# Moving the residual fold of a layernorm from VectorE to ScalarE

## The reference

```python
def _layernorm(x, axis=-1, eps=1e-5):
    m = jnp.mean(x, axis=axis, keepdims=True)
    v = jnp.var(x, axis=axis, keepdims=True)
    return (x - m) / jnp.sqrt(v + eps)
...
    # x: (16, 2048, 2048) float32
    xn = _layernorm(x, axis=-1)
    x = x + _L0_attn_ref(xn, ...) + _L0_ffn_ref(xn, ...)
# attention: q = xn @ Wq; latent = xn @ Wkv; k, v = latent @ Wk, latent @ Wv; 16 heads,
#   each row sees its last 128 keys and the first 16; out @ Wo
# ffn: hidden + sigmoid(xn @ router + bias) * (gelu(xn @ w1 + b1) @ w2 + b2) for the rows of
#   the top K scores; _L0_ffn_ref returns its input xn with that added
```

## Time and profile before

| | |
|---|---|
| runs | median 7160.39 us of 3 (7156.94 to 7164.64) |
| profiled execution | 7139.36 us |
| its span, slowest core (5) | 7137.5 us |
| spans of the 8 cores | 7086.8 to 7137.5 us |
| busy, share of the span | PE 82%, DVE 28%, ACT 14%, POOL 2% |
| mean granted PE clock, by core | 0.862 to 0.866 of full speed |

### The profile page before, as it was taken

One profiled execution on the slowest core, in us unless ns is written; L12 is line 12 of the kernel. 1 busy time (PEld: TensorE's weight loads), 2 busy tenths in 40 slices (PEclk: granted clock), 3 DMA queues, 4 the chain that ended last, 5 costly groups with the idle time before them and its releaser, 6 DMA issues.

```text
span 7137.5 us, 105085 instructions; the slowest of 8 cores (7086.8 to 7137.5 us)
## 1 busy us (share of the span) xinstructions
PE 5835.5 (82%) x37961; PEld 3597.9 (50%) x37961; DVE 1995.4 (28%) x4806; ACT 1028.1 (14%) x2688; POOL 160.1 (2%) x155
## 2 busy tenths in 40 slices
PE   2446675868996899968996899967998789977999
PEld 1124343535664366724674357643765356643667
DVE  2033000145113531136112431136212451135211
ACT  0012000104100211004101120104011031103110
POOL 2101011000000000000000000000000000000000
PEclk8656888986998789986998889986999879987999
DMA  9999999721443234431443224431444214431344
GB/s 117 106 122 121 150 154 129 195 89 57 151 150 128 72 119 151 156 107 59 148 152 133 89 95 150 149 128 41 150 152 160 89 69 151 149 128 60 134 145 160
DMA packets 449713, 885.86 MB, mean 124 GB/s; under 512 B 202880, under 2 KB 305856, under 8 KB 400064
## 3 DMA queue, kind: packets, MB, share of 16 engines
q1 hardware_dynamic: 152864, 587.61, 24.3%
q0 software_dynamic: 268704, 90.20, 14.3%
q10 hardware_dynamic: 27648, 201.34, 8.0%
HBM read 935.69 MB, written 123.73 MB: 148 GB/s over the span
## 4 chain that ended last, share of the span: by engine, by line
PE 66%; DMA 16%; DVE 10%; issue 6%; ACT 1%; DVEq 1%; POOL 0%; SPq 0%; ACTq 0%; POOLq 0%
PE ps_ev L826 12%; PE ps_ev L852 12%; DMA w_s<-w_t 6%; PE ps_sB L826 6%; PE ps_sA L826 6%; PE ps_sB L852 6%; PE ps_sA L852 6%; PE ps_ev L786 3%; DMA wq_s<-wq_t 3%; PE ps_ev L572 3%; DMA wk_s<-wk_t 3%; DVE negmax L683 2%; PE ps_sB L786 1%; PE ps_sA L786 1%; DVE p_sb L703 1%
## 5 line engine op out<-in xcount | busy, mean ns | idle before, releaser
L852 PE MATMUL ps_ev<-w_s,hT 128*128 128x256 bf16 x8192 | 957.7, 276 | 158.2 <-DMA w_s<-w_t 127.3
L863 DVE SCALAR_TENSOR_TENSOR acc<-ps_ev,gcol,acc 128x256 f32<-128x256 f32 x512 | 247.9, 484 | 2638.8 <-PE ps_ev L852 2638.8
L852 PEld LDWEIGHTS ps_ev<-w_s,hT 128*128 128x128 bf16 x8192 | 807.5, 99 | 284.3 <-issue 181.8
L826 PE MATMUL ps_ev<-xnT,w_s 128*128 128x512 bf16 x4096 | 911.2, 381 | 34.9 <-DMA w_s<-w_t 34.7
L826 PEld LDWEIGHTS ps_ev<-xnT,w_s 128*128 128x128 bf16 x4096 | 401.9, 98 | 516.8 <-issue 45.4
L826 PE MATMUL ps_sB<-xnT,w_s 128*128 128x512 bf16 x2048 | 472.5, 385 | 36.3 <-DMA w_s<-w_t 36.3
L838 ACT ACTIVATE hT<-ps_ev,b1T 128x512 bf16<-128x512 f32 x256 | 175.9, 687 | 2229.7 <-PE ps_ev L826 2229.6
L852 PE MATMUL ps_sA<-w_s,hT 128*128 128x256 bf16 x4096 | 489.0, 273 | 0.0
L852 PE MATMUL ps_sB<-w_s,hT 128*128 128x256 bf16 x4096 | 489.0, 273 | 0.0
L826 PE MATMUL ps_sA<-xnT,w_s 128*128 128x512 bf16 x2048 | 466.9, 381 | 18.8 <-DMA w_s<-w_t 18.8
L852 PEld LDWEIGHTS ps_sB<-w_s,hT 128*128 128x128 bf16 x4096 | 400.7, 98 | 46.4
(11 more groups left out here) (172 smaller groups left out, 5858.6 us busy)
## 6 DMA issues: line engine op xcount, KB each, us to landing
w_s<-w_t SPq DMA_DIRECT2D x512, 512.0 KB, 3.9
w_s<-w_t SPq DMA_DIRECT2D x128, 1024.0 KB, 5.7
w_s<-w_t ACTq DMA_DIRECT2D x128, 1024.0 KB, 5.3
wq_s<-wq_t SPq DMA_DIRECT2D x128, 512.0 KB, 3.5
wo_s<-wo_t SPq DMA_DIRECT2D x64, 1024.0 KB, 4.9
w_t<-w POOLq DMA_DIRECT2D x64, 512.0 KB, 39.3
w_t<-w POOLq DMA_DIRECT2D x32, 1024.0 KB, 60.1
y<-acc ACTq DMA_DIRECT2D x32, 1024.0 KB, 5.4
```

The source lines that it names most:

```text
L826: p.do("tensor", lambda e, jj=jj, c=c, bk=bk: e.matmul(ev_ring.bufs[bk][:], R_w1.bufs[jj][:, c, :], xnT[:, c, :], start=(c == 0), stop=(c ...
L852: p.do("tensor", lambda e, jj=jj, c=c, s=s, bk=bk: e.matmul(ev_ring.bufs[bk][:, 0:256], hT[:, c, s * 128:(s + 1) * 128], R_w2.bufs[jj][:, ...
L863: lambda e, sl=sl, s=s, bk=bk: e.scalar_tensor_tensor(acc[:, s, sl * 256:(sl + 1) * 256], ev_ring.bufs[bk][:, 0:256], gcol[:, s:s + 1], ac ...
```

## The change

The fold x * s0c + s1c is done by ACT as an Identity activation with both factors as per-row operands, in place of DVE's `tensor_scalar`. Four things follow from it in the code: `xn_S[u]`, for which PE waits, is now the count after L467 (its line is 466 in the changed kernel; the fold is at line 473); ACT waits for that same count ahead of its fold; the wait for `acc_out_at[0]` stands on ACT ahead of the fold; and `acc_base_S` is the ACT count of the last fold.

```diff
@@ -461,17 +462,18 @@
             mathB_V[u] = p.c["s_V"]
-            if u == 0:
-                p.waitt("vector", acc_out_at[0])
             p.chain("vector", "s_V",
                     lambda e, xa=xa, u=u: e.tensor_scalar(
                         xnb[u][:], xa, rstd[:, u:u + 1], s1c[:, u:u + 1],
                         ALU.mult, ALU.add))
-            p.chain("vector", "s_V",
-                    lambda e, xa=xa, u=u: e.tensor_scalar(
-                        acc[:, u, :], xa, s0c[:, u:u + 1], s1c[:, u:u + 1],
-                        ALU.mult, ALU.add))
             xn_S[u] = ("s_V", p.c["s_V"])
+            p.wait("scalar", "s_V", p.c["s_V"])
+            if u == 0:
+                p.waitt("scalar", acc_out_at[0])
+            p.do("scalar", lambda e, xa=xa, u=u: e.activation(
+                out=acc[:, u, :], in_=xa, func=AF.Identity,
+                scale=s0c[:, u:u + 1], bias=s1c[:, u:u + 1]), inc="s_S")
+            fold_S[u] = p.c["s_S"]
@@ -502,7 +504,7 @@
-        acc_base_S = xn_S[NSUB - 1]
+        acc_base_S = ("s_S", fold_S[NSUB - 1])
```

More of the change, by code:

```diff
@@ L396, in build @@
         xn_S = [0] * NSUB
+        fold_S = [0] * NSUB
         hb = [0]
```

## The result

| | before | changed |
|---|---|---|
| all runs, median | 7230.01 us (36) | 7284.67 us (34) |
| fastest run | 7136.69 us | 7104.64 us |
| ratio of undisturbed runs | | 0.9938, 95% interval 0.9912 to 0.9965 |

In more than half of all executions the cores of one die, sometimes of both, showed a lower granted clock (0.81 for long stretches where others show 1.00) and were up to 12% longer, whatever the kernel, so that kernels are compared here by the ratio and by undisturbed dies alone, those with a mean granted clock of at least 0.857. By the ratio the change makes the kernel 0.6% faster. 14 of the 34 runs lie under 7160 us; their median is 7121.6, and that of the lowest 14 of the 36 runs of before 7159.8.

A forecast was written before the change was run, and what follows sets the result against it. The chain of waits through DVE and PE in the layernorm stage, fold included, was taken to set the end. Seven stages of 4 x 1.455 = 5.82 us give 40.7; 7160.4 - 40.7 = 7119.7, said as 7120, range 7096 to 7141.

The forecast's parts named there:

- The fold on the path, 1.455 us per block: Layernorm stage: with the fold off DVE, PE's transposes begin 1.455 us earlier per block, 5.82 us per stage.
- Seven stages, not eight: Groups 1 to 7 each win 5.82 us, 40.7 in all; group 0 wins 0, hidden by PE's wait for `wq_s`.
- ACT: free: The fold arriving on ACT takes 1.9 us, delays nothing on the path, and costs 0.
- unless it takes some 6.5 us: ACT after block 0: 6.5 us left before block 2's root, so only a fold of about that length would cost.
- No table load: ACT at the folds: Identity should add no table load; even if it did, nothing reaches the path, cost 0.
- A: PE's clock after each stage returns no sooner on the time axis: only 20.4 us won, 7140; chance 0.09.
- B: PE's clock is up as dense work starts: 3.5 us more per stage, 24.5 in all, 7095; chance 0.07.
- C: Groups 1 to 7 wait for weights as group 0 does, so nothing is won: 7160; chance 0.06.
- D: ACT's fold holds up DVE's copies beside it: +12.5 us, 7173, or 7186 with block 3's Square; chance 0.04.
- The time itself: Whole kernel: the median of the runs, 7160.4, less 40.7 gives 7119.7, said as 7120, range 7096 to 7141.

The follow-up runs named there:

- e5: The kernel before with a second fold per block on DVE, to unused memory; 7221.1 us, +38.4 ± 8.9 us against before on undisturbed dies.
- e6b: The kernel before with one copy for four transposes, fold still on DVE; 7058.4 us, -93.8 ± 5.5 us against before, ratio 0.9893.
- e8: The kernel before with three more folds per block on DVE in group 0 only; 7139.9 us, -12.3 ± 3.5 us against before, ratio 0.9994.
- e4: The changed kernel with ACT working out each fold four times, three to unused memory; 7147.4 us, -35.3 ± 10.1 us against before.
- e0: The changed kernel measured once more, no edit; 7104.4 us, -39.4 ± 3.9 us against before on undisturbed dies, ratio 0.9951.
- e7: The changed kernel with one copy for four transposes and block 3's sum over x on ACT; 7024.6 us, -158.1 ± 4.1 us against before.

## Why the prediction was right or wrong

**The fold on the path, 1.455 us per block: right.** 1.50, 1.47, 1.48, 1.42 by block, e5 gives 1.36 to 1.48 for another one, e6b the same price in a shorter stage.

**Seven stages, not eight: right.** 7 x 5.82 = 40.7 was forecast, -39.4 ± 3.9 and a ratio of 0.9938 came (7119.7 / 7160.4 is 0.9943). These alone could not tell seven stages from eight, 46.6 us. What tells is e8, where 17.5 us more in group 0 cost nothing, and the start of group 1, which in the profiled executions did not come earlier.

**ACT: free, right, but its step was mis-sized twice.** The fold takes 2.09 us, not 1.9: it has two per-row operands, the Square none. The Trainium skill, "ScalarE: Activation LUTs", section "What ACT_TABLE_LOAD costs", has 93 ns for each such operand; by it an estimate is 1.895 + 0.186 = 2.08, and the row agrees with 2.093. The type written does not matter: the folds of e4 that write bf16 take 2.093 too. And I asked when a root is queued, not when it is read: it is read one block later, so "unless it takes some 6.5 us" was too tight, as e4 shows with 8.5 us. No table load came at a fold:

```profile
L473 ACT ACTIVATE acc<-acc,s1c,s0c 128x2048 f32<-128x2048 f32 x24 | 50.2, 2093 | 92.7 <-DVE hT L466 92.7
...
L474 ACT ACTIVATE aoT<-acc,s1c,s0c 128x2048 bf16<-128x2048 f32 x72 | 150.7, 2093 | 33.7 <-DVE hT L466 29.2
...
L536 ACT ACT_TABLE_LOAD x8 | 10.3, 1283 | 54.9 <-PE ps_oA L529 54.9
...
L443 ACT ACT_TABLE_LOAD x7 | 9.0, 1283 | 10.8 <-DVE varv L438 10.8
```

These groups of ACT (L474 is e4's, the others the changed kernel's) answer to the earlier trace rows, with the same two counts of loads.

**Rivals.** A and B (the clock) fall by e0: the granted clock returned 6.61 us after the kbuf copy began, 6.55 before; by A it would have come some 6 us later, by B as the dense work began. C falls by the ratio, D by e4: the copies stayed at 225 and 217 ns.

**The time itself: wrong.** 7284.67 us was measured and 7096 to 7141 was the range. The step that failed is the last, "7160.4 - 40.7 = 7119.7 as a median": it took the median of three runs of before, 7156.94 to 7164.64, for the level of the kernel, and the range had no term for long runs. The runs showed in its place 36 times from 7136.69 to 7972.42 with a median of 7230.01, 70 us above the level taken. The other 95 us of the miss are the draw of the changed kernel, whose median came out 55 above that and not 41 below: 20 of its 34 runs lie over 7160 us, so a median falls among the long ones and says little of the kernel. Nor would undisturbed dies alone have fixed the level: on these, before stood at 7143.8, 7182.7 and 7152.2 us on three chips, 39 us apart, as much as the change is worth. The range held the terms of the change and hardly the level. Among the 14 runs under 7160 the median, 7121.6, is what was forecast.

## What to carry to other kernels

Read from the stage's timeline whether the instruction stands in the string that the next stage waits for, not from an engine's share: an engine busy 28% of the span was the path here, and each microsecond off it came out once per block in the groups where nothing covered it. Any place off that string will do, another engine or, where a gap is wide enough, the same one a few microseconds later; and before work is moved, look at the string's other members: four large copies for sixteen small ones gave 2.9 us per block, twice what the fold gave. Forecast the difference from one profile, but take the level, and its range, from many runs.

## What the runs showed of the hardware

- A PSUM to SBUF copy of bf16 on DVE takes 0.22 us for 128 columns and 0.42 for 512: four times the data in less than twice the time.
- ACT working without a break beside DVE's copies (e4) changed them by nothing that the rows show, 225 and 217 ns against 225 and 217.
- The granted PE clock came back 6.3 to 6.6 us after the start of the kbuf copy, where dense work begins, as a mean of each version's stages (single stages 4.4 to 8.3), although the stretch at 0.50 around it was 67.7 us long before and 48.3 in e7.
- An Identity on ACT with two per-row operands over 2048 columns took 2.093 us, whether it wrote float32 or bf16; the Square without such operands 1.895.
- The same kernel took 7143.8, 7152.2 and 7182.7 us on undisturbed dies of three chips, 0.5% apart.
